# Setup's last stretch of an attention kernel rewritten: key sums with memberships as weights, feature sums on TensorE

## The chip, the cores and the metric

The kernel is one program on one core of a Trainium2 chip. The metric is the device time of that core in microseconds (us). TensorE is called PE, VectorE DVE, ScalarE ACT, GpSimd POOL in the profile; SP issues the transfers. The program is written with explicit semaphores: an engine runs its own instructions in program order, and `wait_ge` holds it until another engine has counted a semaphore up.

## What is computed

A cross-attention block without softmax, then a self-attention block with one; the change is in what the first of them needs once for all rows. Cut to that (H = 8 heads of D = 128, DIM = 256, 32 batches, 256 query rows and 77 context rows in each):

```python
def proj(t):                                   # LayerNorm, then w_in, split in heads
    return heads(layer_norm(t, ln_g, ln_b) @ w_in.T)
f_q, f_k, f_v = proj(q), proj(k), proj(v)      # q: the rows of x, normalized; k = v: the context
k_ratio = 2.0 * jnp.minimum(k_var, 1.0) / (k_var + 1.0)   # k_var: variance over D of a row of f_k
q_flat = (f_q - f_q.mean(-1, keepdims=True)).reshape(H, -1, D)
feat_corr = jnp.einsum('hnd,hne->hde', q_flat, q_flat) / q_flat.shape[1]
decorr_scale = jnp.exp(-5.0 * norm(offdiagonal(feat_corr)) / (D * D))
feats = jnp.concatenate([f_q.mean(axis=(1, 2)), f_k.mean(axis=(1, 2))], axis=-1)
h1 = jnp.maximum(layer_norm(feats @ wp_w1.T + wp_b1, wp_ln_g, wp_ln_b), 0.0)
weights = jax.nn.softmax(h1 @ wp_w2.T + wp_b2, axis=-1)     # three mixing weights for a head
mixed = cw * cosine_sim + vw * cosine_sim * decorr_scale + ww * q_ratio * k_ratio
x = x + jnp.tanh(g_xattn[0]) * (mixed @ f_v @ w_out.T + b_out)
```

## The kernel before

The program has a setup phase and a main phase, two blocks one after the other; the main phase is the same before and after. Setup reads all of x and of the context once, in NG = 4 steps. In a step PE turns the normalized context rows (tile cz, in 5 tiles of 128 rows, CG = 5), ScalarE and VectorE make their fp16 halves (cTh, cTl), PE projects them (`products`: three fp16 matmuls for one fp32 one, high times high, high times low, low times high), VectorE takes the statistics of each head (fst) and from them the ratio that goes into kst; then PE adds 16 tiles of normalized x rows to the gram matrix (gram_ps, with a column of ones that gives the sums of x).

The last stretch of the setup follows those four steps. On each engine it is one list in program order. Its parts:

- wmean and wcT: w_in with the mean of each head's 128 columns taken off (VectorE, L444 to L446).
- krm (L462): for each context row its ratio, spread over the 8 batches of a step and zero where the row isn't of that batch; member is that 0 or 1. 64 columns for a tile of 128 rows (8 batches by 8 heads).
- zs, sums, spread (L476 to L483): the column sums of x and of the context; spread puts them on all 128 columns as weights, so that PE's product with the identity gives them on every partition (L749).
- gram (L487 to L502): the gram matrix with ln_g and ln_b worked in, its lower block ("lower") turned by PE (L753).
- wof: product of two later weights (PE L742, VectorE L505).
- fe, the feature sums (L511 to L515): a multiply of w_in with the spread sums and a reduction, for x and for the context.
- hm = gram x wcT (PE L763), and from it the correlations of four heads each (PE L782, VectorE L532 to L535).
- h1, h1T, logits, dgw, mix: the small network on fe, and its softmax.
- key sums (PE L815, L818): for each batch and head the sum of normalized context rows times ratio. kz is this with ln_g and ln_b, kzTh and kzTl its fp16 halves; "key values" (L861 to L863 on wT and kzT) and the out products (on ku and woutT) follow, and kr goes to HBM as its two halves krh and krl.
- `split_rest(n)`: the low fp16 half of wN, wq, wk, wv and woutT on VectorE (L471), after ScalarE's high half (L642).

PE counts `pe_step` up at each turn, and the other engines wait for its values. The key sums of before take the data as weights:

```python
nc.tensor.matmul(gram_ps[0][:, k * NB * H + i * SB * H:k * NB * H + (i + 1) * SB * H],
                 cz[:, i * CG + t, k * P:(k + 1) * P], weights[t], start=(t == 0), stop=(t == CG - 1))
```

The second argument is the operand that is loaded (128 x 128 here), the third the one that streams (64 columns here), and fp32 matmuls run as two passes, which the profile counts as two instructions.

Of the kernel before, what the change touches and what calls it, by code (L numbers as in the profile page):

```python
# [48 lines left out]
def bc(ap, shape):  # L49
    return ap.to_broadcast(shape)  # L50
# [37 lines left out]
def setup_phase(nc, ctx, w, a):  # L88
# [22 lines left out]
    cz = sb("s_cz", [P, NG * CG, DIM])  # L111
# [20 lines left out]
    spread = sb("s_spread", [P, 2, KT, P])  # L132
# [23 lines left out]
    with ExitStack() as summed:  # L156
        wsum = summed.enter_context(nc.sbuf_tensor("s_wsum", [P, H, DIM], F32))
# [18 lines left out]
    wT_half, wT_split, w_half, w_gated, wof_half = sem("s_wTh"), sem("s_wTs"), sem("s_wh"), sem("s_wg"), sem("s_wofh")  # L176
# [10 lines left out]
    with nc.Block() as block:  # L187
        @block.sync
        def _(sp):
# [25 lines left out]
            with nc.allow_non_contiguous_dma(reason="columns of a few values"):  # L215
# [39 lines left out]
                sp.wait_ge(kr_act, 4)  # L255
# [8 lines left out]
        def _(pool):  # L264
# [14 lines left out]
            nc.gpsimd.memset(fixed[:, 1, 1, :], 0.0).then_inc(consts, 1)  # L279
            nc.gpsimd.memset(member[:], 1.0).then_inc(member_ready, 1)  # L280
            pool.wait_ge(member_ready, 1)
            full_rows, last_rows = member[:, 0:CG - 1, :], member[:, CG - 1, :]
            for n, (rows, pattern, base, sign) in enumerate((
# [5 lines left out]
                pool.wait_ge(member_ready, n + 2)  # L289
# [41 lines left out]
        def _(dve):  # L331
# [94 lines left out]

            dve.wait_ge(wT_half, 1)
# [3 lines left out]
            with dve.Fori(0, NG - 1) as i:  # L431
                count = [0]

                def in_loop(_, ins):
# [9 lines left out]
            link(nc.vector.tensor_reduce(wmean[:], full["wT"][:].rearrange("p k (h d) -> p (k h) d", d=DH), AX.X, ALU.add))  # L444
            link(nc.vector.tensor_scalar(wmean[:], wmean[:], -1.0 / DH, None, ALU.mult))
            link(nc.vector.tensor_tensor(wcT[:].rearrange("p k (h d) -> p (k h) d", d=DH),  # L446
                                         full["wT"][:].rearrange("p k (h d) -> p (k h) d", d=DH),
                                         bc(wmean[:].unsqueeze(2), [P, KT * H, DH]), ALU.add))
            assert done[0] == DVE_LOOPS
            dve.wait_ge(ct_full, NG * CG + START)  # L450
            nc.vector.tensor_reduce(sums[:, :, 1], csums[:].rearrange("p n k -> p k n"), AX.X, ALU.add)
# [3 lines left out]
            link(nc.vector.tensor_scalar(tb[:], tb[:], w["tg"][0:1, 0:1], FV, ALU.mult, ALU.mult))  # L455
            link(nc.vector.tensor_copy(fixed[:, 0, 0, :], tb[:]))
            nc.vector.tensor_tensor(fixed[:, 0, 1, :], tb[:], fixed[:, 0, 0, :], ALU.subtract).then_inc(fixed_ready, 1)
            dve.wait_ge(member_ready, 6)
            dve.wait_ge(rk_ready, 2 * NG + START)
# [5 lines left out]
            last.then_inc(kr_dve, 1)  # L465

            def split_rest(n):
# [7 lines left out]
            dve.wait_ge(pe_step, 1)  # L475
# [4 lines left out]

            for j in range(2):
                for k in range(KT):
                    last = nc.vector.tensor_scalar(spread[:, j, k, :], ones[:], sums[:, k, j:j + 1], None, ALU.mult)  # L483
# [4 lines left out]
            link(last)  # L488
# [4 lines left out]
            dve.wait_ge(pe_step, 3)  # L493
# [7 lines left out]
            dve.wait_ge(pe_step, 4)  # L501
# [8 lines left out]
            for j in range(2):  # L510
                link(nc.vector.tensor_tensor(wsum[:], full["wN"][:], bc(t_ps[0][:, j * DIM:(j + 1) * DIM].unsqueeze(1),  # L511
                                                                        [P, H, DIM]), ALU.mult))
                link(nc.vector.tensor_reduce(fe[:, j, :], wsum[:], AX.X, ALU.add))
            nc.vector.tensor_scalar(fe[:, 0, :], fe[:, 0, :], 1.0 / ROWS, None, ALU.mult)
            tail_link("fe", nc.vector.tensor_scalar(fe[:, 1, :], fe[:, 1, :], 1.0 / CROWS, None, ALU.mult))  # L515
            split_rest(0)

            dve.wait_ge(pe_step, 8)
            link(nc.vector.tensor_tensor(h1[:], t_ps[1][0:H, 0:DH], rows8[:, 0, :], ALU.add))
            link(nc.vector.bn_stats(h1s[:], h1[:]))  # L520
            link(nc.vector.bn_aggr(h1v[:, 0:2], h1s[:]))
            tail_link("h1var", nc.vector.tensor_scalar(h1v[:, 1:2], h1v[:, 1:2], EPS, None, ALU.add))
            dve.wait_ge(pool_step, 3)
# [3 lines left out]
            tail_link("h1", nc.vector.tensor_scalar(h1[:], h1[:], 0.0, None, ALU.max))  # L527

# [57 lines left out]
        def _(act):  # L586
# [1107 lines left out]
```

## Time and profile before

| | us |
|---|---|
| median of 3 runs | 1452.59 (1451.85 to 1452.68) |
| the profiled execution | 1452.54 |
| its span, first to last instruction | 1450.8 |
| PE busy | 1305.6 (90%) |
| VectorE busy | 1138.5 (78%) |
| ScalarE busy | 1023.9 (71%) |
| GpSimd busy | 199.1 (14%) |

Busy shares are those of the whole span. The setup is its first seventh, so the time of the change is to be read from that stretch alone: which engine the others wait for there, and when.

### The profile page before, as it was taken

How to read it: one execution, taken by the hardware profiler on the slowest of the kernel's cores; microseconds unless marked ns; L12 is line 12 of the kernel's file. 1: busy time of each engine (PE TensorE's matmuls, PEld its weight loads, DVE VectorE, ACT ScalarE, POOL GpSimd, SP SyncE). 2: the span in 40 equal slices, each digit the busy share in tenths (PEclk: the TensorE clock that was granted, in tenths of full speed). 3: DMA queues.
4: the chain of work that ended last, by engine and by line, in shares of the span. 5: the costliest groups of instructions: out<-in, count | busy, mean ns of one | idle time of the engine just before them, and what ended most of it. 6: DMA issues, size and time to landing. Idle time of an engine off the chain costs nothing.

```text
span 1450.8 us, 35577 instructions
## 1 busy us (share of the span) xinstructions
PE 1305.6 (90%) x10818; PEld 878.3 (61%) x10818; DVE 1138.5 (78%) x3171; ACT 1023.9 (71%) x3381; POOL 199.1 (14%) x128
## 2 busy tenths in 40 slices
PE   4998838799999999999999999999999999999955
PEld 2565636566666666666666666666666666666621
DVE  5777545578888889888879787979787979797854
ACT  5565113368787878787878787878787878786866
POOL 2343041010202020202020202020202020202000
PEclk9999969899999999999999999999999999999987
DMA  8430001050606060605050505151515141514130
GB/s 265 140 109 18 1 13 46 26 160 5 170 11 166 15 164 16 162 19 160 21 156 25 156 25 147 33 151 30 147 34 142 38 140 41 136 44 130 39 117 15
DMA packets 151433, 124.52 MB, mean 86 GB/s; under 512 B 14462, under 2 KB 139039, under 8 KB 151392
## 3 DMA queue, kind: packets, MB, share of 16 engines
q1 hardware_dynamic: 151392, 124.00, 30.8%
q8 instruction: 22, 0.36, 0.1%
q14 instruction: 19, 0.16, 0.0%
HBM read 87.00 MB, written 25.77 MB: 78 GB/s over the span
## 4 chain that ended last, share of the span: by engine, by line
PE 38%; DVE 18%; issue 14%; ACT 6%; DMA 5%; SPq 3%; DVEq 1%; POOL 1%; ACTq 0%; POOLq 0%
PE work L861 10%; PE work L863 10%; PE work L862 10%; DVE nm L1627 5%; DMA sqE<-sq_rows 4%; PE attended L1347 4%; ACT prob L1437 3%; DVE mTl L1537 3%; PE score L1335 2%; SPq L1180 2%; DVE md L1582 2%; PE work L1242 1%; DVE l2s L1597 1%; DVE norm L1607 1%; DVE norm L1518 1%
## 5 line engine op out<-in xcount | busy, mean ns | idle before, releaser
L1437 ACT ACTIVATE prob<-score,nm 128x256 f32<-128x256 f32 x1024 | 473.2, 480 | 44.6 <-DVE nm L1627 40.4
L1627 DVE TENSOR_REDUCE nm<-score 128x2 f32<-128x512 f32 x512 | 340.2, 683 | 22.2 <-PE score L1335 20.0
L1437 ACT ACTIVATION_READ_ACCUMULATOR prob<-score,nm 128x1 f32 x1024 | 216.7, 212 | 0.0
L1335 PE MATMUL score<-qstack,kstack 128*128 128x256 f16 x1024 | 186.0, 277 | 28.4 <-ACT prob L1437 19.2
L1550 DVE BATCH_NORM_STATS2 qst<-work 128x6 f32<-128x128 f32 x512 | 112.6, 285 | 77.0 <-PE work L863 77.0
L1347 PE MATMUL attended<-prob,vsp 128*32 128x256 f32 x2048 | 139.4, 390 | 4.0 <-DVE vsp L1641 3.2
L1335 PEld LDWEIGHTS score<-qstack,kstack 128*128 128x128 f16 x1024 | 86.6, 98 | 87.7 <-ACT prob L1437 55.5
L861 PE MATMUL work<-woutTh,fvph 128*128 128x256 f16 x384 | 105.0, 273 | 13.7 <-DVE Vpl L1525 12.7
L1482 POOL TENSOR_TENSOR rq<-qft,mhalf 128x32 f32<-128x32 f32 x16 | 86.8, 5428 | 197.0 <-DVEq L1557 197.0
L1422 ACT ACTIVATE v<-work 128x512 f32<-128x512 f32 x32 | 19.1, 597 | 130.4 <-PE work L863 130.4
L862 PE MATMUL work<-woutTl,fvph 128*128 128x256 f16 x384 | 104.7, 273 | 0.0
L863 PE MATMUL work<-woutTh,fvpl 128*128 128x256 f16 x384 | 104.7, 273 | 0.0
L1486 POOL TENSOR_TENSOR l2r<-l2v,mhalf 128x4 f32<-128x4 f32 x16 | 16.1, 1008 | 608.6 <-DVE l2v L1600 608.6
L861 PE MATMUL work<-wTh,xTh 128*128 128x512 f16 x256 | 97.0, 379 | 2.8 <-DVE ql L1537 1.4
L863 PE MATMUL work<-wTh,xTl 128*128 128x512 f16 x256 | 97.0, 379 | 0.0
L862 PE MATMUL work<-wTl,xTh 128*128 128x512 f16 x256 | 97.0, 379 | 0.0
L861 PE MATMUL work<-xTh,Gh 128*128 128x256 f16 (+1 forms) x320 | 88.9, 278 | 6.2 <-DVE md L1582 5.8
L862 PE MATMUL work<-xTl,Gh 128*128 128x256 f16 (+1 forms) x320 | 88.5, 277 | 0.0
L863 PE MATMUL work<-xTh,Gl 128*128 128x256 f16 (+1 forms) x320 | 88.4, 276 | 0.0
L1347 PEld LDWEIGHTS attended<-prob,vsp 128*32 128x32 f32 x2048 | 53.9, 110 | 56.9 <-DVE vsp L1641 17.4
L861 PE MATMUL work<-Vph,mTh 128*128 128x256 f16 (+1 forms) x320 | 87.5, 273 | 0.1
L863 PE MATMUL work<-Vph,mTl 128*128 128x256 f16 (+1 forms) x320 | 87.1, 272 | 0.0
(324 smaller groups left out, 3398.4 us busy)
## 6 DMA issues: line engine op xcount, KB each, us to landing
kstack<-parts SPq DMA_DIRECT2D x256, 64.0 KB, 2.9
qstack<-parts SPq DMA_DIRECT2D x256, 64.0 KB, 2.9
sqE<-sq_rows SPq DMA_DIRECT2D x64, 154.0 KB
s_xin<-in_x SPq DMA_DIRECT2D x8, 1024.0 KB, 6.0
xin<-in_x SPq DMA_DIRECT2D x16, 512.0 KB, 6.7
x2S<-in_x SPq DMA_DIRECT2D x16, 512.0 KB, 7.7
x<-x2S SPq DMA_DIRECT2D x16, 512.0 KB, 3.4
out<-zb SPq DMA_DIRECT2D x16, 512.0 KB, 3.4
```

The lines of the kernel that those rows point to most:

```text
L861: nc.tensor.matmul(out, a["h"][at], b["h"][bt], start=first, stop=False)
L862: nc.tensor.matmul(out, a["h"][at], b["l"][bt], start=False, stop=False)
L863: return nc.tensor.matmul(out, a["l"][at], b["h"][bt], start=False, stop=last)
L1180: sp.dma_start(sqE[lo:hi, t, :], sq_rows[h, :].partition_broadcast(hi - lo)).then_inc(sq_in, 16)
L1335: last = nc.tensor.matmul(sc[n % SC][:, jj * NQ:(jj + 1) * NQ], kstack[:, e, j, b2 * NQ + k * P:b2 * NQ + (k + 1) * P], qstack[:, j, b2 * ...
L1347: last = nc.tensor.matmul(pvb[t][32 * j:32 * j + 32, 0:NQ], vsp[:, e, k, j, :], prob[:, n % PG, k, j, :], start=(e == 0 and k == 0), stop= ...
L1437: nc.scalar.activation(prob[:, g % PG, k, u % 4, :], sc[n % SC][:, jj * NQ:(jj + 1) * NQ], ACT.Exp, bias=nm[:, u:u + 1], accum_out=sums[:, ...
L1482: nc.gpsimd.tensor_tensor(rq[:], qft[:, 0, :, :], w["mhalf"][:].rearrange("p (t h) -> p t h", h=H), ALU.pow).then_inc(rq_ready, 1)
L1537: ins = nc.vector.scalar_tensor_tensor(dst, src, scale, emptied(e, "h")[0], ALU.mult, ALU.subtract)
L1550: last = nc.vector.bn_stats(qst[:, t, 4 * half + h, :], bank(e)[:, h * DH:(h + 1) * DH])
L1582: drain(nc.vector.tensor_tensor(md[0:r, c % 2, 0:n * 2 * P].rearrange("p (t n) -> p t n", n=2 * P), bank(e)[0:r, 0:n * 2 * P].rearrange("p ...
L1627: nc.vector.tensor_reduce(nm[:, 2 * n:2 * n + 2], sc[n % SC][:, :].rearrange("p (u q) -> p u q", q=NQ), AX.X, ALU.max, negate=True).then_i ...
```

## The change

- The key sums exchange their operands: krm (64 columns) is loaded, and cz streams with 256 columns and a 257th of ones, which gives the sum of the ratios that the products with `ones` gave. The result has batches and heads on the partitions, so the gains come in as a row (g_bc, b_bc) on VectorE, and four transposes (kzT) follow. The sums come in two parts: one before hm in the first gram bank, one behind hm in the second.
- The feature sums are PE matmuls: w_in loaded, the two columns of sums streamed. VectorE only scales them. Spread keeps its half for x.
- The gate tanh(g) goes into the scale of woutT's two halves (tgw), and VectorE's multiply of woutT goes.
- wmean and wcT are made ahead of the four steps, before wTl.
- The order in the last stretch is new on all engines; krm no longer waits for the norms that GpSimd makes.

```diff
@@ VectorE, ahead of the four steps @@
+            dve.wait_ge(early, 16 * N_EARLY)
+            link(nc.vector.tensor_reduce(wmean[:], full["wT"][:].rearrange("p k (h d) -> p (k h) d", d=DH), AX.X, ALU.add))
+            link(nc.vector.tensor_scalar(wmean[:], wmean[:], -1.0 / DH, None, ALU.mult))
+            link(nc.vector.tensor_tensor(wcT[:].rearrange("p k (h d) -> p (k h) d", d=DH),
+                                         full["wT"][:].rearrange("p k (h d) -> p (k h) d", d=DH),
+                                         bc(wmean[:].unsqueeze(2), [P, KT * H, DH]), ALU.add))
             dve.wait_ge(wT_half, 1)
...
@@ VectorE, last stretch @@
-            dve.wait_ge(act_step, 1)
-            nc.vector.tensor_scalar(full["woutT"][:], full["woutT"][:], w["tg"][:, 0:1], None, ALU.mult).then_inc(w_gated, 1)
...
-            dve.wait_ge(rk_ready, 2 * NG + START)
...
-                nc.vector.scalar_tensor_tensor(w[name]["l"][:], full[name][:], WS, w[name]["h"][:], ALU.mult, ALU.subtract)
+                nc.vector.scalar_tensor_tensor(w[name]["l"][:], full[name][:], tgw[:, 0:1] if name == "woutT" else WS,
+                                               w[name]["h"][:], ALU.mult, ALU.subtract)
...
+            dve.wait_ge(pe_step, PE_TAIL["fe"])
+            means = t_ps[1][:, DIM:DIM + 2 * H].rearrange("p (h j) -> p j h", j=2)
+            nc.vector.tensor_scalar(fe[:, 0, :], means[:, 0], 1.0 / ROWS, None, ALU.mult)
+            tail_link("fe", nc.vector.tensor_scalar(fe[:, 1, :], means[:, 1], 1.0 / CROWS, None, ALU.mult))
+            dve.wait_ge(pe_step, PE_TAIL["lower"])
             tail_link("lower", nc.vector.tensor_copy(gram[:, 1, 0:P], t_ps[1][:, 0:P]))
...
-                link(nc.vector.tensor_reduce(fe[:, j, :], wsum[:], AX.X, ALU.add))
...
+            dve.wait_ge(kr_act, 2)
+            link(nc.vector.tensor_tensor(kz[:], krs[:, :, 0:DIM], bc(g_bc[:].unsqueeze(1), [P, 2, DIM]), ALU.mult))
+            for n in range(2):
+                last = nc.vector.scalar_tensor_tensor(kz[:, n, :], b_bc[:], krs[:, n, DIM:DIM + 1], kz[:, n, :],
                                                       ALU.mult, ALU.add)
             last.then_inc(kr_dve, 1)
...
@@ ScalarE @@
+            def keep_keys(n):
+                act.wait_ge(pe_step, PE_TAIL[f"keys{n}"])
+                nc.scalar.activation(krs[:, n, :], gram_ps[n][:, 0:DIM + 1], ACT.Copy).then_inc(kr_act, 1)
...
@@ PE @@
+            for h in range(H):
                 for k in range(KT):
+                    last = nc.tensor.matmul(t_ps[1][:, DIM + 2 * h:DIM + 2 * h + 2], full["wT"][:, k, h * DH:(h + 1) * DH],
+                                            sums[:, k, :], start=(k == 0), stop=(k == KT - 1))
+            reached("fe", last)
+
+            def key_sums(n):
+
+                for half in range(2):
+                    i = 2 * n + half
+                    for t in range(CG):
+                        last = nc.tensor.matmul(gram_ps[n][half * SB * H:(half + 1) * SB * H, 0:DIM + 1],
+                                                krm[:, i * CG + t, :, :].rearrange("p b h -> p (b h)"),
+                                                cz[:, i * CG + t, :], start=(t == 0), stop=(t == CG - 1))
+                reached(f"keys{n}", last)
+
+            pe.wait_ge(kr_dve, 1)
+            pe.wait_ge(step, DVE_TAIL["gramg"])
+            key_sums(0)
+            pe.wait_ge(step, DVE_TAIL["fe"])
+            reached("lower", nc.tensor.transpose(t_ps[1][:, 0:P], gram[:, 0, P:DIM], w["ident"][:]))
...
+            key_sums(1)
```

Where the instructions stand shows in the order of each engine (out<-in, shape of the result, xcount of matmuls, not passes). PE before, from the last gram matmul to the start of the second part of the key sums:

```order
L742 MATMUL s_fps<-s_wff,s_woT 128x256 x4
L749 MATMUL s_tps<-ident,s_spread 128x128 x4
L753 MATMUL s_tps<-ident,s_gram 128x128
L763 MATMUL s_fps<-s_wcT,s_gram 128x512 x8
L768 MATMUL s_fps<-ident,s_kst 16x128 x8
L793 MATMUL s_tps<-s_w1T,s_fe 8x128 x2
L782 MATMUL s_gram<-s_hm,s_wcT 128x128 x8
L798 MATMUL s_tps<-ident,s_h 128x8
L782 MATMUL s_gram<-s_hm,s_wcT 128x128 x8
L802 MATMUL s_tps<-s_w2T,s_h1T 8x3
L768 MATMUL s_fps<-ident,s_kst 16x128 x8
L815 MATMUL s_gram<-s_krm,s_cz 128x64 x10
```

PE after, the same place:

```order
L746 MATMUL s_fps<-s_wff,s_woT 128x256 x4
L752 MATMUL s_tps<-ident,s_spread 128x128 x2
L756 MATMUL s_tps<-s_sums,s_wT 128x2 x16
L765 MATMUL s_gram<-s_cz,s_krm 64x257 x10
L774 MATMUL s_tps<-ident,s_gram 128x128
L776 MATMUL s_tps<-s_w1T,s_fe 8x128 x2
L787 MATMUL s_fps<-s_wcT,s_gram 128x512 x8
L765 MATMUL s_gram<-s_cz,s_krm 64x257 x10
L793 MATMUL s_fps<-ident,s_kst 16x128 x8
L816 MATMUL s_tps<-ident,s_h 128x8
L807 MATMUL s_gram<-s_hm,s_wcT 128x128 x8
L821 MATMUL s_tps<-s_w2T,s_h1T 8x3
```

The feature sums (s_sums, s_wT) and the first key sums (s_cz, s_krm) now stand ahead of the hm matmuls (s_wcT, s_gram), the second ones behind them, and h1's matmul ahead of hm.

VectorE before, at the end of the four steps, from wmean to the gram's first operation:

```order
L444 TENSOR_REDUCE s_wmean<-s_wT 128x16
L445 TENSOR_SCALAR s_wmean<-s_wmean 128x16
L446 TENSOR_TENSOR s_wcT<-s_wT,s_wmean 128x2048
L451 TENSOR_REDUCE s_sums<-s_csums 128x2
L454 TENSOR_SCALAR s_woutT<-s_woutT,tg 128x2048
L455 TENSOR_SCALAR s_tb<-s_tb,tg 1x256
L456 CAST s_fixed<-s_tb 1x256
L457 TENSOR_TENSOR s_fixed<-s_tb,s_fixed 1x256
L462 TENSOR_TENSOR s_krm<-s_kst,s_member 128x320 x4
L476 COPY s_zs<-s_gram 128x1
```

VectorE after, at the start of the setup, from the first shift to the first x statistics:

```order
L356 SCALAR_TENSOR_TENSOR s_cnm<-s_cmv,s_crs 128x5
L428 TENSOR_REDUCE s_wmean<-s_wT 128x16
L429 TENSOR_SCALAR s_wmean<-s_wmean 128x16
L430 TENSOR_TENSOR s_wcT<-s_wT,s_wmean 128x2048
L434 SCALAR_TENSOR_TENSOR wTl<-s_wT,wTh 128x2048
L361 BN_STATS s_xst<-s_xin 128x6 x8
```

The wmean and wcT operations went from the first place to the second, ahead of wTl.

VectorE before, from the second correlation to the out products:

```order
L546 TENSOR_REDUCE s_lg<-s_lg 8x1
L548 COPY s_dec<-s_tps 128x8
L471 SCALAR_TENSOR_TENSOR wkl<-s_wk,wkh 128x512
L553 SCALAR_TENSOR_TENSOR s_kz<-s_fps,bcol,s_kz 128x256 x2
L557 RECIPROCAL s_lg<-s_lg 8x1
L558 TENSOR_SCALAR s_lg<-s_lg 8x3
L560 TENSOR_SCALAR s_dgw<-ident,s_lg 8x8 x3
L471 SCALAR_TENSOR_TENSOR wvl<-s_wv,wvh 128x512
L471 SCALAR_TENSOR_TENSOR woutTl<-s_woutT,woutTh 128x2048
L566 TENSOR_TENSOR s_kzTl<-s_kz,s_kzTh 128x512
L568 SCALAR_TENSOR_TENSOR wofl<-s_wo,wofh 128x2x256
```

VectorE after, from the second correlation to the out products:

```order
L523 TENSOR_TENSOR s_fc<-s_gram,s_off 128x512
L525 TENSOR_TENSOR s_fc<-s_fc 128x512
L526 TENSOR_REDUCE s_fcs<-s_fc 128x4
L545 SCALAR_TENSOR_TENSOR s_kzTl<-s_fps,s_kzTh 128x512
L548 RECIPROCAL s_lg<-s_lg 8x1
L549 TENSOR_SCALAR s_lg<-s_lg 8x3
L551 TENSOR_SCALAR s_dgw<-ident,s_lg 8x8 x3
L554 COPY s_dec<-s_tps 128x8
L466 SCALAR_TENSOR_TENSOR wvl<-s_wv,wvh 128x512
L466 SCALAR_TENSOR_TENSOR woutTl<-s_woutT,s_tgw,woutTh 128x2048
L558 SCALAR_TENSOR_TENSOR s_kul<-s_fps,s_kuh 128x256
```

The split of wk and the kz operation are gone from here (they stand ahead of the correlations now), kzTl stands ahead of the softmax tail and of the splits, and kul right behind woutTl.

## Rows read from the trace of the kernel before

**Rows 1.** Timeline of GpSimd at the change of phase: start, us, engine, line, operation
```profile
203.50 2.93 POOL L1469 MEMSET fvph<- 128x3391 f16 x1 [19.71 <-POOLq L187]
```

**Rows 2.** Windows: us; busy us and count of PE, PEld, DVE, ACT, POOL; clock; DMA
```profile
160.00:180.00 20.00, 17.43 (x142) 16.84 (x142) 7.20 (x19) 1.01 (x1) 0.54 (x1) 0.91 0.01 1
```

**Rows 3.** Timeline of ScalarE (ACT), start of the setup
```profile
12.18 1.91 ACT L589 ACTIVATE wTh<-s_wT 128x2048 f16<-128x2048 f32 x1 [10.09 <-DMA s_bbc<-in_ln_b]
```

**Rows 4.** Timeline of VectorE (DVE), start of the setup
```profile
14.13 2.29 DVE L428 SCALAR_TENSOR_TENSOR wTl<-s_wT,wTh 128x2048 f16<-128x2048 f32 x1 [4.52 <-ACT wTh L589]
16.34 2.70 DVE L361 BATCH_NORM_STATS2 s_xst<-s_xin 128x6 f32<-128x256 f32 x8
```

**Rows 5.** Timeline of PE in the setup; a bracket is idle time and releaser
```profile
33.20 0.38 PE L861 MATMUL s_fps<-wTh,s_cTh 128*128 128x512 f16 x1 [1.11 <-DVE s_fst L379]
...
139.23 0.92 PE L735 MATMUL s_gram<-s_zeros 1*128 1x257 f32 x4
140.08 1.99 PE L742 MATMUL s_fps<-s_wff,s_woT 128*128 128x256 f32 x8
...
163.05 3.60 PE L782 MATMUL s_gram<-s_hm,s_wcT 128*128 128x128 f32 x16
...
167.59 2.34 PE L815 MATMUL s_gram<-s_krm,s_cz 128*128 128x64 f32 x20
169.77 1.28 PE L818 MATMUL s_fps<-s_krm,s_ones 128*128 128x64 f32 x10
...
187.49 0.22 PE L861 MATMUL s_fps<-s_kzTh,wTh 128*128 128x32 f16 x1 [2.92 <-DVE s_kzTl L566]
...
191.53 0.40 PE L861 MATMUL s_fps<-woutTh,s_kuh 128*32 128x256 f16 x1 [1.00 <-DVE s_kul L579]
```

**Rows 6.** Timeline of VectorE, last stretch of the setup
```profile
133.18 2.28 DVE L444 TENSOR_REDUCE s_wmean<-s_wT 128x16 f32<-128x2048 f32 x1
...
135.71 2.29 DVE L446 TENSOR_TENSOR s_wcT<-s_wT,s_wmean 128x2048 f32<-128x2048 f32 x1
...
140.36 1.68 DVE L462 TENSOR_TENSOR s_krm<-s_kst,s_member 128x320 f32<-128x320 f32 x4
141.97 0.14 DVE L476 COPY s_zs<-s_gram 128x1 f32<-128x1 f32 x1
...
148.16 2.29 DVE L511 TENSOR_TENSOR s_wsum<-s_wN,s_tps 128x2048 f32<-128x2048 f32 x1
...
162.88 0.69 DVE L532 TENSOR_TENSOR s_fc<-s_gram,s_off 128x512 f32<-128x512 f32 x1
...
182.98 0.14 DVE L557 RECIPROCAL s_lg<-s_lg 8x1 f32<-8x1 f32 x1
...
184.54 2.29 DVE L471 SCALAR_TENSOR_TENSOR woutTl<-s_woutT,woutTh 128x2048 f16<-128x2048 f32 x1
186.74 0.69 DVE L566 TENSOR_TENSOR s_kzTl<-s_kz,s_kzTh 128x512 f16<-128x512 f32 x1
...
191.05 0.42 DVE L579 SCALAR_TENSOR_TENSOR s_kul<-s_fps,s_kuh 128x256 f16<-128x256 f32 x1 [2.44 <-ACT s_kuh L677]
198.76 2.28 DVE L582 SCALAR_TENSOR_TENSOR s_krl<-s_fps,s_krh 32x2048 f16<-32x2048 f32 x1 [7.29 <-ACT s_krh L680]
```

**Rows 7.** Windows of the last stretch; the third number from the end is the clock
```profile
142.00:146.20 4.20, 1.23 (x9) 0.97 (x8) 3.96 (x17) 0.60 (x1) 0.00 (x0) 1.00 0.00 0
149.93:154.65 4.72, 4.72 (x13) 2.09 (x12) 4.65 (x3) 1.02 (x1) 0.00 (x0) 1.00 0.00 0
163.30:166.70 3.40, 3.40 (x18) 3.16 (x17) 2.51 (x6) 0.00 (x0) 0.00 (x0) 0.50 0.01 2
167.50:180.90 13.40, 13.40 (x123) 13.40 (x121) 1.59 (x4) 1.01 (x1) 0.00 (x0) 1.00 0.01 1
187.50:190.50 3.00, 3.00 (x48) 2.85 (x48) 1.04 (x5) 0.00 (x0) 0.00 (x0) 0.50 0.00 0
191.50:196.70 5.20, 5.17 (x24) 3.45 (x24) 0.00 (x0) 0.00 (x0) 0.00 (x0) 0.50 0.00 0
```

More of the change, by code:

```diff
@@ L775, in turn_keys @@
                         last = turn_stats(f_ps[0:2 * H, i, t * P:(t + 1) * P], i, t)
-                last.then_inc(pe_step, 1)
+                reached(f"turned{n}", last)
             def correlate(a):
@@ L840, in _ @@
             for i in range(NG):
                 last = turn_stats(gram_ps[1][0:2 * H, i * P:(i + 1) * P], i, CG - 1)
-            last.then_inc(pe_step, 1)
-            pe.wait_ge(step, DVE_TAIL["dgw"])
-            nc.tensor.matmul(t_ps[0][:, 0:3 * H], ones[0:H, :], dgw[:].rearrange("p a h -> p (a h)"),
-                             start=True, stop=True).then_inc(pe_step, 1)
-            key_values()
+            reached("last", last)
+            pe.wait_ge(kr_dve, 3)
+            for h in range(H):
+                for k in range(KT):
+                    rows = {half: kzT[half][:, k, :].rearrange("p (b h) -> p b h", h=H) for half in "hl"}
+                    last = products(nc, f_ps[:, 1, h * NB:(h + 1) * NB], w["wT"], (ALL, k, slice(h * DH, (h + 1) * DH)),
+                                    rows, (ALL, ALL, h), k == 0, k == KT - 1)
@@ new lines, in _ @@
+            last.then_inc(kr_pe, 1)
+            pe.wait_ge(step, DVE_TAIL["dgw"])
+            pe.wait_ge(step, DVE_TAIL["dec"])
+            reached("mix", nc.tensor.matmul(t_ps[0][:, 0:3 * H], ones[0:H, :], dgw[:].rearrange("p a h -> p (a h)"),
+                                            start=True, stop=True))
+            pe.wait_ge(kr_dve, 4)
+            pe.wait_ge(kT_ready, 2)
+            for h in range(H):
+                last = products(nc, f_ps[0:NB, h // 2, h % 2 * DIM:(h % 2 + 1) * DIM], ku, (ALL, h), w["woutT"], (ALL, h))
@@ L850 @@
+            last.then_inc(kr_pe, 1)
 STEP_LINKS = 4 + 8 + 7
 DVE_LOOPS = 4 + 3 + NG * STEP_LINKS - 4
-_TAIL = ["bias", "biash", "zs", "zg", "sums", "spread", "gramg", "gramb", "bu", "gram", "lower", "wof", "wx", "xmean", "wc", "cmean", "fe",
-         "h1add", "h1bn", "h1aggr", "h1var", "h1norm", "h1g", "h1b", "h1", "fcmask0", "fcsq0", "fcsum0", "h1T",
-         "fcmask1", "fcsq1", "fcsum1", "ladd", "lmax", "dec", "lrec", "lscale", "dgw"]
+_TAIL = ["zs", "zg", "sums", "spread", "gramg", "gramb", "bu", "gram", "fe", "lower", "wof",
+         "h1add", "h1bn", "h1aggr", "h1var", "h1norm", "h1g", "h1b", "h1", "h1T", "kzg", "fcmask0", "fcsq0", "fcsum0",
+         "ladd", "lmax", "fcmask1", "fcsq1", "fcsum1", "lrec", "lscale", "dgw", "dec"]
@@ L855 @@
 DVE_TAIL = {name: DVE_LOOPS + 1 + n for n, name in enumerate(_TAIL)}
+_TURNS = ["gram", "wof", "spread", "fe", "keys0", "lower", "h1", "hm0", "hm1", "keys1", "turned0", "h1T", "corr0", "logits",
+          "corr1", "turned1", "kzT", "norms", "last", "mix"]
+PE_TAIL = {name: 1 + n for n, name in enumerate(_TURNS)}
 def products(nc, out, a, at, b, bt, first=True, last=True):
```

222 lines of the change are left out of this document (95 added, 127 removed).

## The prediction

> **What bounds the kernel now.** The change lies wholly in the setup, the first 203.5 of 1450.8 us; the main phase after it begins only when setup's last store has landed (GpSimd's first memset of it, 203.50 [rows 1]), so what setup gains or loses moves the rest as a block. I then read the busy time by stretch: between 160 and 180 us PE is busy 17.43 of 20 us and VectorE 7.20 [rows 2], so PE is the bound there. The timelines then give the order. The tail begins where PE ends the gram matrix (L735) at about 140.08 [rows 5]; VectorE is late for it and touches it at 141.97, behind krm [rows 6]. Then VectorE is the bound for the feature sums (four operations of 2.29 us from 148.16) and PE for the key sums from 167.59 to 180.9, and the reader is to see that VectorE then still has two splits to do (182.98 to 186.74) before kzTl, which releases the first key-values matmul at 187.49. The out products start at 191.53 behind kul. Everything behind that point (24 products, krh, krl, the store) stays as it is, so I build the new start of the out products and compare it with 191.53.
>
> **The front, which gets longer.** The wcT block (L444 to L446: 2.28, about 0.2 and 2.29 us, 4.8 in all [rows 6]) goes ahead of wTl. The weights are there at 12.18, when ScalarE starts wTh [rows 3]; VectorE idles until 14.13 and then makes wTl [rows 4]. Now it works from 12.18 to 17.0 and wTl starts at 17.0: 2.9 us late. Is that absorbed? Behind wTl on VectorE stand the row statistics of the first x block (16.34), on which the normalization, the lowers and so PE wait; PE itself waits for VectorE at 33.20 [rows 5]. I see no wait on a transfer between, so I take all 2.9; the bounds are 0 (all absorbed) and 4.8 (nothing of the block hidden). The loops and the gram's end come 2.9 later, at 142.98.
>
> **The hand-over to the tail.** On VectorE the block (4.8), the gate of woutT and the fixed rows (all of them between 133.18 and krm's start at 140.36) go from in front of krm; krm itself is 1.68 [rows 6] and needs no reciprocal norms from GpSimd any more. It is done by about 138, so VectorE now waits for the gram: it starts at 143.1 and not at 141.97, 1.1 us later than before. ScalarE's woutTh now starts 10 us earlier; nothing waits for it, since its split is the last, so that is worth nothing here.
>
> **PE's queue in the tail.** A full 128-column fp32 weight load with few moving columns costs one pass 0.11 us (167.59 to 169.77 is 20 passes, twice 0.11 for each fp32 matmul [rows 5]). A pass of 512 columns costs 0.43 us at full clock (11 starts in 4.72 us [rows 7]), and one of 256 at most 0.25 (8 in 1.99 [rows 5]); for the new passes of 257 columns I take 0.22, between half of 0.43 and 0.25.
> Removed: 120 passes, 13.4 us, of the old key sums [rows 5, 7], and of the spread half its passes. Added: the feature sums, 16 matmuls = 32 passes of 2 columns, 3.5 us; the key sums in two parts of 20 passes, 4.4 us each; four transposes. The 2-column pass is not in the trace: the nearest from below is 0.06 us (the fp16 key-values products, 48 from 187.49 in 3.0 us [rows 5, 7]), which gives 1.9 us; from above the slow-clock pass of L782, 16 in 3.60 or 0.225 [rows 5], which gives 7.2. It loads the same fp32 weights as L815, so 0.11.
> PE then runs without a wait that I can find: wof 1.9, feature sums 3.5, first key sums 4.4, the hm matmuls 16 x 0.43 = 6.9, second key sums 4.4, first correlation 16 x 0.11 = 1.8, and 18 small passes (spread, lower, h1, the turned keys, h1T) 2.0. The sum is 24.9, with 0.3 for hand-overs 25.2: 168.2. VectorE's gram work, 4.5 us, hides under PE's feature sums and first key sums; wNl (2.3 us) and two small splits hide under hm. If PE's stretch were shorter than about 14 us, those would show.
>
> **Then VectorE again.** Two correlations of three 0.69 us operations [rows 6], the logits between (0.3) and kzTl 0.7 make 5.2: 173.4, with hand-overs 173.9. kz (about 1.6: three operations of the 0.69 us kind and shorter) fits before the first correlation, since the second key sums end at about 165.4. Key-values products start at 174.0 and not at 187.49. Behind kzTl stand the softmax tail and one split (182.98 to 184.54, 1.6), the copy of dec 0.2 and woutTl 2.2 (184.54 to 186.74) [rows 6]: 177.9. PE needs 3.0 us for the products and ScalarE 0.4 for kuh, 177.5, so kul waits for woutTl by 0.4. With kul's 0.42 the out products start at 178.5. Against 191.53 that is **13.0 us** of gain at full clock, the front's 2.9 us already taken off.
> The DMA of the reciprocal norms now goes out some 3 us earlier and the fixed rows with it, both long before krh; they cost nothing.
>
> **The clock.** PE's granted clock is 0.50 in 3.40 us from 163.30, 1.00 from 167.50 to 180.90, and 0.50 again in both last product stretches [rows 7]. It fell after stretches such as 142.0 to 146.2, where PE was busy 1.23 of 4.20 us. Of the stretch from 187.5 to 190.5 PE counts 3.00 busy, with 32-column matmuls, and stays at 0.50. The new feature sums are 3.5 us of passes with 2 columns, less array work than any of these. I hold it likelier than not that the clock falls once by them, and that 3.4 us of work then run at 1.2 GHz: half of 3.4, 1.7 us, is lost. Gain 13.0 - 1.7 = 11.3. The last products are taken at 0.50 as before.
> The Trainium skill, page TensorE: Matmul & The Clock Gate, section What's actually happening, says that the gate is set by how busy PE has been, and that activity releases it. Taken by PE's busy time the feature sums would count as work and the clock would stay up: the sum would be 13.0 and not 11.3. The trace's 187.5 stretch, busy and yet at 0.50, does not bear that reading out, but no row shows a fall under it.
>
> **Rivals.**
> (A) The clock holds through the feature sums: 1452.6 - 13.0 = **1439.6**. For it: it holds over 13.4 us of 64-column key sums. 30%.
> (B) The front's 2.9 us are absorbed in the loops: 1452.6 - 15.9 = 1436.7, or 1438.4 with one fall. Against it: PE waits for VectorE in each block. 7%.
> (C) The last products run at full clock, because PE's wait before the key-values products (2.92 us for kzTl [rows 5]) becomes shorter: half of 5.2 us comes off, 1438.7 with one fall. Against it: the 32-column products stand before them as they did, and no rise came then. 9%.
> (D) The clock falls twice or more, or the 257-column passes cost as much as two (8.8 us more): 1443 to 1450. 11%.
> (E) Slower: the feature sums put the clock down and the key sums, whose weights fill half of the columns, do not bring it back. From 145.4 to 173 PE has some 25 us of work at full clock; each us of it done at 0.50 costs one more. It decides from 13.0 us of such work on, and with all of it the time is 1452.6 + 12 = 1464.6. For it: 5.2 us at 0.50 from 191.5 with 256 columns. Against it: it rose at 166.7 and held through 64 columns [rows 7]. 3%.
>
> **How the numbers follow.** The profiled run took 1452.54 us, the median of the runs is 1452.59, so differences of the trace hold for the median. The forecast (one fall, 40%) is 1452.6 - 11.3 = 1441.3 us. Range: down to (B) and (C) without their tails, 1437.0, and up into (D), 1446.0. Within 0.2% (2.9 us) is about what a measurement of this kernel can't tell from no change. Faster by more: all cases but (E) and the end of (D), 0.95; the same 0.02; slower 0.03.
>
> **What would show it.** The second VectorE wTl at 17 us; L735 ending near 143; a granted clock of 0.50 for one stretch within 146 to 154; PE without idle from 145 to 170; VectorE idle about 5 us before the gram and again before h1T; the first key-values matmul near 174 (176 with a fall) and the first out product near 178.5 (180). It would be wrong if 257-column passes cost far over 0.22, if VectorE's waits in the reordered tail (it now waits for lower only behind the key sums, with wof, h1 and wNl queued behind) reach PE, or if the loops take up the front's delay.

## The result, and the profile after

The changed kernel took 1435.99 us in the median of 4 runs (1433.1 to 1438.16), the kernel before 1452.22 (1448.39 to 1452.68): ratio 0.9893, 95% interval 0.9868 to 0.9917, so 12.1 to 19.2 us faster. Over all later runs too the means are 1452.8 us (43 runs, standard deviation 2.4) and 1437.4 us (13 runs, 2.7): 15.4 us, with a standard error of 0.8. The forecast was 1441.3, between 1437.0 and 1446.0. The direction and the mechanism in the setup were right; the time came out 1.0 us below the range.

The profiled execution took 1433.1 us, its span is 1431.4. GpSimd's timeline of it shows the end of the setup, where before it was at 203.50 [rows 1]:

```profile
188.03 2.93 POOL L1479 MEMSET fvph<- 128x3391 f16 x1 [13.17 <-POOLq L186]
```

So 15.5 us of the 19.4 by which the two spans differ come from the setup, and 3.9 from the main phase, whose program is the same.

VectorE's timeline of the front, for [rows 4]:

```profile
12.29 2.29 DVE L428 TENSOR_REDUCE s_wmean<-s_wT 128x16 f32<-128x2048 f32 x1 [2.41 <-DMA s_bbc<-in_ln_b]
...
17.15 2.29 DVE L434 SCALAR_TENSOR_TENSOR wTl<-s_wT,wTh 128x2048 f16<-128x2048 f32 x1
19.36 2.70 DVE L361 BATCH_NORM_STATS2 s_xst<-s_xin 128x6 f32<-128x256 f32 x8
```

The block runs from 12.29, and wTl starts 3.0 us later than before, as forecast (2.9).

VectorE's timeline of the last stretch, for [rows 6]:

```profile
133.43 1.70 DVE L455 TENSOR_TENSOR s_krm<-s_kst,s_member 128x320 f32<-128x320 f32 x4
135.04 0.19 DVE L460 TENSOR_REDUCE s_sums<-s_csums 128x2 f32<-128x40 f32 x1
140.25 0.16 DVE L470 COPY s_zs<-s_gram 128x1 f32<-128x1 f32 x1 [5.02 <-PE s_gram L739]
...
146.24 0.15 DVE L496 TENSOR_SCALAR s_fe<-s_tps 128x8 f32<-128x8 f32 x1
151.74 0.29 DVE L498 COPY s_gram<-s_tps 128x128 f32<-128x128 f32 x1 [5.35 <-PE s_tps L774]
...
170.91 0.69 DVE L545 SCALAR_TENSOR_TENSOR s_kzTl<-s_fps,s_kzTh 128x512 f16<-128x512 f32 x1 [0.19 <-ACT s_kzTh L665]
...
173.28 2.34 DVE L466 SCALAR_TENSOR_TENSOR woutTl<-s_woutT,s_tgw,woutTh 128x2048 f16<-128x2048 f32 x1
175.54 0.41 DVE L558 SCALAR_TENSOR_TENSOR s_kul<-s_fps,s_kuh 128x256 f16<-128x256 f32 x1
```

krm is done at 135, then VectorE waits 5.0 us for the gram, and 5.4 us for lower behind the feature sums. kul follows woutTl without a gap.

PE's timeline of the last stretch, for [rows 5]:

```profile
139.29 0.92 PE L739 MATMUL s_gram<-s_zeros 1*128 1x257 f32 x4
...
142.41 3.63 PE L756 MATMUL s_tps<-s_sums,s_wT 128*128 128x2 f32 x32
145.97 5.40 PE L765 MATMUL s_gram<-s_cz,s_krm 128*64 128x257 f32 x20
...
152.10 7.13 PE L787 MATMUL s_fps<-s_wcT,s_gram 128*128 128x512 f32 x16
159.16 3.74 PE L765 MATMUL s_gram<-s_cz,s_krm 128*64 128x257 f32 x20
...
171.66 0.22 PE L871 MATMUL s_fps<-s_kzTh,wTh 128*128 128x32 f16 x1
...
176.01 0.40 PE L871 MATMUL s_fps<-woutTh,s_kuh 128*32 128x256 f16 x1 [0.76 <-DVE s_kul L558]
```

PE runs without a gap from the gram to the second correlation. The first key sums take 5.4 us and the second 3.7, with the same 20 passes. The last gram matmul starts at 139.29, and not 2.9 us behind the 139.23 of before. From there to the first out product are 36.7 us, where [rows 5] give 52.3.

Windows of the changed kernel; the clock is the third number from the end, for [rows 7]:

```profile
142.50:145.90 3.40, 3.40 (x33) 3.40 (x31) 1.81 (x6) 0.27 (x1) 0.00 (x0) 1.00 0.02 5
147.40:150.70 3.30, 3.30 (x13) 1.96 (x12) 0.00 (x0) 0.00 (x0) 0.00 (x0) 0.50 0.00 0
159.30:162.80 3.50, 3.50 (x20) 2.12 (x19) 0.00 (x0) 0.99 (x1) 0.00 (x0) 1.00 0.00 0
176.00:181.00 5.00, 4.99 (x24) 3.43 (x24) 2.01 (x8) 0.00 (x0) 0.00 (x0) 0.50 0.12 16
```

The 32 two-column passes run at full clock; 1.3 us behind them the clock falls to 0.50 for 3.4 us, within the first key sums. The second key sums run at 1.00, and the out products at 0.50 as before.

### The profile page after: what moved, and what is told of

Same layout as the page of the kernel before. It is cut to its first block, busy times and chain, and to the rows that moved or that the text cites. A ratio compares the mean times of both kernels' runs of the same rounds, so it can differ in the third digit from the quotient of the medians.

```text
span 1431.4 us, 35480 instructions
## 1 busy us (share of the span) xinstructions
PE 1296.1 (91%) x10770; PEld 870.6 (61%) x10770; DVE 1127.5 (79%) x3165; ACT 1022.2 (71%) x3382; POOL 200.7 (14%) x129
## 4 chain that ended last, share of the span: by engine, by line
PE 39%; DVE 18%; issue 14%; ACT 6%; DMA 5%; SPq 2%; DVEq 1%; POOL 1%; ACTq 0%; POOLq 0%
PE work L871 11%; PE work L873 11%; PE work L872 11%; DVE nm L1637 6%; DMA sqE<-sq_rows 4%; PE attended L1357 4%; ACT prob L1447 3%; DVE mTl L1547 2%; PE score L1345 2%; SPq L1190 2%; DVE md L1592 2%; PE work L1252 1%; DVE l2s L1607 1%; DVE norm L1617 1%; DVE norm L1528 1%
## 5 line engine op out<-in xcount | busy, mean ns | idle before, releaser
L1447 ACT ACTIVATION_READ_ACCUMULATOR prob<-score,nm 128x1 f32 x1024 | 220.6, 215 | 0.0
```

What stands on the lines that cost most here:

```text
L1447: nc.scalar.activation(prob[:, g % PG, k, u % 4, :], sc[n % SC][:, jj * NQ:(jj + 1) * NQ], ACT.Exp, bias=nm[:, u:u + 1], accum_out=sums[:, ...
```

## The experiments

**Where the front's delay went.** The gram's last matmul came at the same time in both first profiles, though everything in front of it began 2.9 us late. Four runs ask why: both kernels again, the block put back in the changed kernel, and the block alone moved in the kernel before.

The block (wmean and the operations after it to wcT) put back (wc_back), its first two operations shown:

```diff
-            dve.wait_ge(early, 16 * N_EARLY)
-            link(nc.vector.tensor_reduce(wmean[:], full["wT"][:].rearrange("p k (h d) -> p (k h) d", d=DH), AX.X, ALU.add))
-            link(nc.vector.tensor_scalar(wmean[:], wmean[:], -1.0 / DH, None, ALU.mult))
...
             dve.wait_ge(wT_half, 1)
...
             tiles(NG - 1, straight, False)
+            link(nc.vector.tensor_reduce(wmean[:], full["wT"][:].rearrange("p k (h d) -> p (k h) d", d=DH), AX.X, ALU.add))
+            link(nc.vector.tensor_scalar(wmean[:], wmean[:], -1.0 / DH, None, ALU.mult))
...
             assert done[0] == DVE_LOOPS
```

The block alone moved (front_only) is the same edit the other way round, in the kernel before.

> The kernel before, unchanged, for a second profile. Theory 1 (the granted clock's slow stretches in the four steps fall where they fall by chance in each execution, and that hid the front's 2.9 us): the steps' total time at clock 0.50 differs from the first profile's 17 us, and the end of the gram (L735) moves with it, by up to 3 us to either side of 139.2. Theory 2 (the delay of the front itself moves the steps to where the clock falls less): the total is 17 us again and L735 starts within 0.5 us of 139.2.

> The changed kernel, unchanged, for a second profile and a time. Theory 1: L739 starts somewhere from 139 to 143.5, in step with the time at clock 0.50 in the four steps (6.9 us in the first profile). Theory 2: 139.3 again. Either way VectorE is idle behind krm until the gram, and the first out product comes 36 to 38 us behind L739's start (36.7 in the first profile). Time 13 to 17 us below the kernel before.

> The changed kernel with the three wmean/wcT operations put back behind the four steps, where VectorE was idle for 5.0 us: they take 4.8 there. Theory 1 (the front costs its 2.9 us, hidden in the first profile by chance): 2.9 us faster than after_again in the median of the rounds, wTl starts at about 14.1. Theory 2 (the front costs nothing or the later start even helps): the same time as after_again or up to 3 us slower.

> The kernel before with only the three wmean/wcT operations moved ahead of wTl. VectorE then reaches the gram about 2 us sooner than PE ends it, so PE's end binds. By theory 1: steps 2.9 us later, VectorE's lateness at the gram (1.8 us) gone: 1.1 us slower than the kernel before. By theory 2: 1.8 us faster, or more. VectorE idle for about 3 us in front of the gram only if it is freed of the block.

Windows of the four steps, first of the kernel before in its first profile, then of before_again, then of front_only:

```profile
16.00:136.00 120.00, 107.07 (x517) 66.91 (x518) 91.58 (x415) 75.20 (x206) 41.80 (x19) 0.93 0.41 129
```

```profile
16.00:136.00 120.00, 105.08 (x534) 68.06 (x535) 94.01 (x417) 75.00 (x205) 44.65 (x19) 0.97 0.41 128
```

```profile
16.00:136.00 120.00, 102.28 (x517) 65.37 (x518) 93.97 (x418) 76.69 (x207) 41.70 (x19) 0.97 0.41 129
```

PE's timeline at the last gram matmul of before_again and of front_only:

```profile
136.38 0.92 PE L735 MATMUL s_gram<-s_zeros 1*128 1x257 f32 x4
```

```profile
139.29 0.92 PE L736 MATMUL s_gram<-s_zeros 1*128 1x257 f32 x4
```

With the clock at a mean of 0.97 in both, the block in front costs 139.29 - 136.38 = 2.9 us. The first profile of the kernel before had 0.93 there: 17.1 us at 0.50, by windows of 1 us added up, against 6.8 in before_again. It is the odd one in where the gram ends: six profiles of the kernel before have the last gram matmul at 139.23, 136.38, 136.81, 136.60, 136.66 and 136.80, five of the changed kernel at 139.29, 138.65, 138.64, 139.49 and 138.81. The means are 137.1 and 139.0; without the odd one the front costs 2.3 us. It is not absorbed in the steps, or by 0.6 us at most. Theory 1 stands in its main point, that the first profile of before hid the delay by chance. But the end of the gram does not simply move with the time at 0.50: with the same code in the steps it came at 136.28 both in wc_back (3.4 us at 0.50) and in filled_turns (10.3 us), at 136.66 in before_p5 (10.3 us). It was late only in the first profile of before (17.1 us, 139.23) and in mixed (13.6 us, 138.25), and these two alone of the nine profiles with that code have 6.8 us at 0.50 in one piece, at 57 to 64 us. That this piece is the cause is not shown.

wc_back has the block where VectorE was idle, as its VectorE timeline shows (block, then the gram's first operation):

```profile
130.22 2.28 DVE L444 TENSOR_REDUCE s_wmean<-s_wT 128x16 f32<-128x2048 f32 x1
...
137.23 0.16 DVE L469 COPY s_zs<-s_gram 128x1 f32<-128x1 f32 x1 [0.37 <-PE s_gram L738]
```

Its last gram matmul starts at 136.28, but the feature and key sums then met 6.8 us at 0.50, where the first profile of the changed kernel had 3.4. Its time was 1441.11 us in the median, 0.9909 of before (0.9886 to 0.9933), against 1437.87 and 0.9902 (0.9879 to 0.9925) for after_again. Theory 1 asked for 2.9 us less and the median is 3.2 us more, so by its time this expectation failed; the two intervals overlap almost wholly, and the run can't tell 2.9 us either way. front_only took 1454.97, 1.0014 of before (0.9994 to 1.0034); theory 1 asked for 1.1 us more, which lies inside (so does no change at all), and theory 2's 1.8 us less lies outside. In its profile setup ends at 200.95, where the kernel before, without its odd profile, has 199.9 in the mean, which agrees with theory 1. VectorE is less late there, and not in time: krm still waits 3.65 us for GpSimd's norms, and the hm matmuls start 6.3 us behind the last gram matmul's start, where before had 7.6.

**What the feature sums cost, and what drops the clock.** One kernel (fe_wide, the diff) streams 64 columns where 2 were streamed; the other (fe_one) has the same edit with `range(1)` for `range(H)`, so only the first head's four passes are left:

```diff
             for h in range(H):
                 for k in range(KT):
-                    last = nc.tensor.matmul(t_ps[1][:, DIM + 2 * h:DIM + 2 * h + 2], full["wT"][:, k, h * DH:(h + 1) * DH],
-                                            sums[:, k, :], start=(k == 0), stop=(k == KT - 1))
+                    last = nc.tensor.matmul(t_ps[1][:, DIM:DIM + 64], full["wT"][:, k, h * DH:(h + 1) * DH],
+                                            spread[:, k, 0:64], start=(k == 0), stop=(k == KT - 1))
```

> The changed kernel, with the feature sums' 16 matmuls streaming 64 columns (of the spread sums of x) where 2 were streamed; the sums of single heads and of the context are left out, so its output is not the reference's. Its weight loads stay, so a pass stays at 0.11 us and the 32 take 3.6. If the 2-column passes are what drops the clock (it fell 1.3 us behind their end in the first profile, 3 us behind their start in the second), there is no stretch at 0.50 between 142 and 152, and the first key sums take 3.7 us like the second. If it is something else (the gap ahead, chance), the stretch stays and the first key sums take 5 us or more.

> The changed kernel with one head's feature sum in place of eight: 14 of the 16 matmuls are left out, so its output is not the reference's. If PE's queue binds from the gram to the second key sums, as the prediction's sum has it, the way from the last gram matmul's start to the first out product is shorter by 28 passes x 0.11 = 3.1 us, and by 1.7 more if the clock then holds: 36.7 becomes 33.6 or 31.9. If VectorE's gram work or its splits bound it instead, less than 1.5 us comes off.

PE's timeline and windows of fe_wide:

```profile
142.26 3.68 PE L756 MATMUL s_tps<-s_spread,s_wT 128*128 128x64 f32 x32
145.87 3.75 PE L765 MATMUL s_gram<-s_cz,s_krm 128*64 128x257 f32 x20
```

```profile
142.30:145.80 3.50, 3.50 (x34) 3.50 (x32) 1.85 (x6) 0.31 (x1) 0.00 (x0) 1.00 0.02 5
145.90:149.50 3.60, 3.60 (x21) 2.24 (x20) 0.24 (x2) 0.00 (x0) 0.00 (x0) 1.00 0.00 0
```

The same 32 passes take the same 3.6 us (PEld, the weight load, is busy in all of the 3.50 us with 64 columns as in all of the 3.40 with 2, so it sets the pace, 0.11 a pass), the clock stays at 1.00, and the first key sums take 3.7 us. From the last gram matmul to the first out product are 35.1 us. In all eight profiles in which the 2-column passes stand in one run (five of the changed kernel, one each of wc_back, keys_turns and filled_turns) the clock fell within or just behind them: for 3.4 us in four of them, for 6.8 in the other four. fe_wide is one profile; in fe_one, and in mixed below, no such run of passes is left, and the clock did not fall there either. In fe_one the way from the last gram matmul to the first out product is 32.0 us:

```profile
142.10 0.56 PE L756 MATMUL s_tps<-s_spread,s_wT 128*128 128x64 f32 x4
142.59 3.75 PE L765 MATMUL s_gram<-s_cz,s_krm 128*64 128x257 f32 x20
```

That is 3.1 us shorter than in fe_wide for 28 passes less: PE's queue bounds this stretch, as the sum had it.

**The key sums' passes.** 257 columns were taken at 0.22 us a pass; 20 take 3.7 us, 0.185. They are ten passes on output partitions 0 to 63 and then ten on 64 to 127. An order in which the halves take turns tests that:

```diff
-                for half in range(2):
-                    i = 2 * n + half
-                    for t in range(CG):
+                for t in range(CG):
+                    for half in range(2):
+                        i = 2 * n + half
```

> The changed kernel with the two halves of each key sum taking turns (tile by tile) where they came one after the other. In the profiles 20 passes took 3.7 us at full clock, with starts 0.2 us apart at both ends and 0.07 where the second half (output partitions 64 to 127) follows the first (0 to 63). If passes on different column halves run side by side, and only those of one half wait for each other, each key sum takes about 20 x 0.11 = 2.2 us: 1.5 us less for each, 3 us for both, with PE bound there. If the order doesn't matter, 3.7 us again and no change.

PE's timeline of keys_turns:

```profile
146.87 4.01 PE L765 MATMUL s_gram<-s_cz,s_krm 128*64 128x257 f32 x20
...
158.68 2.40 PE L765 MATMUL s_gram<-s_cz,s_krm 128*64 128x257 f32 x20
```

The second key sums, at full clock, take 2.4 us instead of 3.7, 0.12 a pass: passes on different halves of the output partitions overlap more than those on one half. In both orders a single pass is recorded with 0.38 us. (The Trainium skill, page TensorEngine Tiling (Array Packing), section Key Properties, says that different tiles can execute weight loads and matmuls in parallel; the 0.12 us a pass agrees.) The first take 4.0 in spite of a slow stretch of 3.4 us (5.4 in the changed kernel). The way is 34.0 us. The time, 1436.65 us or 0.9887 (0.987 to 0.9903), is that of the changed kernel within its interval.

**All of it together.** filled_turns has the turns, the block back behind the steps, and the splits of wv and woutT in front of the wait for lower:

```diff
+            split_rest(3)
+            split_rest(4)
             dve.wait_ge(pe_step, PE_TAIL["lower"])
...
-            split_rest(3)
-            split_rest(4)
             dve.wait_ge(kr_act, 4)
```

> The changed kernel with the halves in turns, the wmean/wcT operations back behind the four steps (VectorE idle 5.0 us there) and the splits of wv and woutT moved from behind the softmax tail to where VectorE waits for lower (5.4 us idle). By the sum: 2.9 (front) + up to 3.0 (key sums) + 0.4 (kul no longer waits for woutTl) = 6 us faster than the changed kernel. Two things can eat it: the splits (2.8 us) may reach past lower once the first key sums are 1.5 us shorter, and the clock's slow stretches, worth about 1.7 us each, fall by chance.

Its VectorE timeline: the block, the gram's first operation, woutTl and kul:

```profile
130.23 2.28 DVE L444 TENSOR_REDUCE s_wmean<-s_wT 128x16 f32<-128x2048 f32 x1
...
137.24 0.16 DVE L469 COPY s_zs<-s_gram 128x1 f32<-128x1 f32 x1 [0.35 <-PE s_gram L738]
...
144.03 2.35 DVE L465 SCALAR_TENSOR_TENSOR woutTl<-s_woutT,s_tgw,woutTh 128x2048 f16<-128x2048 f32 x1
...
169.66 0.42 DVE L557 SCALAR_TENSOR_TENSOR s_kul<-s_fps,s_kuh 128x256 f16<-128x256 f32 x1 [2.59 <-ACT s_kuh L666]
```

The idle 5.0 us are used up but for 0.35, and kul waits for kuh alone. The first out product is at 170.1 and setup ends at 181.5 (186.7 to 189.9 in five profiles of the changed kernel). The time is 1432.07 us, 0.9861 of before (0.9843 to 0.988): the lowest median of all, 4.6 us below keys_turns and 3.9 below the changed kernel's 1435.99. Against the changed kernel's mean over all 13 runs, 1437.4, its mean of 4 is 5.3 us lower with a standard error of 1.3, near the expected 6. The intervals of the two ratios overlap (0.9868 to 0.988), so that it beats the changed kernel is likely, not certain.

**A miss.** mixed deals the feature sums' passes out between the key tiles, so that no run of narrow passes is left (its `key_tile(0, h)` is one key matmul, halves in turns, and `key_sums(0, H)` makes the rest); the two waits of the key sums move ahead of the feature sums with it, and otherwise it is filled_turns:

```diff
+            for h in range(H):
+                key_tile(0, h)
                 for k in range(KT):
...
             reached("fe", last)
...
-            key_sums(0)
+            key_sums(0, H)
```

> filled_turns with the feature sums' matmuls dealt out between the tiles of the first key sums: four 2-column passes, then a key tile of two 257-column passes, and so on, the last two tiles behind them. The passes are the same ones. If the run of 2-column passes is what drops the clock, it now stays at 1.00 from the gram to the second key sums and the way from the last gram matmul's start to the first out product is 1.7 us shorter than in filled_turns (33.9): 32.2. If the key tiles no longer overlap one another between the narrow passes, up to 1.4 us of that is lost again: 33.6. By time: 1 to 2 us below filled_turns (0.986 of before), which the rounds may not tell.

The moved waits cost little: PE starts 3.21 us behind the last gram matmul's start, against 3.13 in filled_turns.

Its PE timeline, first four groups, and its windows:

```profile
141.46 0.65 PE L756 MATMUL s_gram<-s_cz,s_krm 128*64 128x257 f32 x2
142.04 0.61 PE L770 MATMUL s_tps<-s_sums,s_wT 128*128 128x2 f32 x4
142.58 0.65 PE L756 MATMUL s_gram<-s_cz,s_krm 128*64 128x257 f32 x2
143.16 0.61 PE L770 MATMUL s_tps<-s_sums,s_wT 128*128 128x2 f32 x4
```

```profile
142.30:145.80 3.50, 3.50 (x22) 2.29 (x21) 1.00 (x3) 0.00 (x0) 0.00 (x0) 1.00 0.00 0
145.90:149.50 3.60, 3.60 (x20) 2.33 (x21) 0.00 (x0) 0.00 (x0) 0.00 (x0) 1.00 0.02 5
```

The clock stays at 1.00, as expected. But a key tile of two passes and four narrow passes now take 1.12 us together (142.58 - 141.46), where four weight-bound passes and two in turns would take 4 x 0.11 + 2 x 0.12 = 0.68. The way is 36.4 us against 33.9 in filled_turns, and the upper expectation of 33.6 was too low as well. Of the 0.44 us more in each group 0.13 is the lost overlap of the halves (a key tile's two passes are one matmul on one half; by the times of the two orders that is 2 x 0.185 = 0.37 and not 0.24); 0.31 is left. A further 0.30 us, once, is PE's wait for lower in the hm matmuls. (The Trainium skill, page TensorEngine Tiling (Array Packing), section Key Properties, says that a change of tiling mode drains TensorE; each group here has two such changes, and the 0.31 us that are left would fit that. No run isolates both; in fe_one the four passes and the change to 64-column weights take 0.49 us, only 0.05 more than 4 x 0.11.) It took 1434.75 us, 0.9864 (0.9846 to 0.9881).

**The main phase.** Its share of the gain was open, so more profiles of the two kernels were taken, with no edit.

> The kernel before, a third profile. In the first two the last gram matmul starts at 139.23 (17 us at clock 0.50 in the four steps) and 136.38 (6.8 us). If the first was the odd one, and 136.4 is where the kernel usually is, this one gives 136.3 to 137.0 and a first out product at 188.6 to 189.3; if both are common, either. The main phase behind setup took 1247.3 and 1249.6 us and should lie between 1243 and 1253.

> The kernel before, a fourth profile, with the same expectation as the third: last gram matmul at 136.3 to 137.0 if the first profile was the odd one.

> The changed kernel, a third profile. Last gram matmul at 138.7 to 139.3 (2.4 to 2.9 us behind the usual one of before), first out product 36.7 us later with one slow stretch in the first key sums. Main phase: 1243.4 us and 1248.2 in the first two; if the first was chance, about 1249.

> The kernel before, a fifth profile. Main phase (from GpSimd's first memset of it to the end) 1250 us if the new setup shortens it, 1248 to 1249 as the common mean if it is scatter; single profiles scatter by 2.5 us, so only the means over all of them count. Setup ends at 199.4 to 199.7 in three of four.

> The kernel before, a sixth profile, expectation as for the fifth.

> The changed kernel, a fourth profile. Main phase 1246 if it is shorter behind the new setup, 1248 to 1249 if that was scatter. Setup ends at 186.7 to 188.9.

> The changed kernel, a fifth profile, expectation as for the fourth.

From each profile: the start of GpSimd's first memset of the main phase, and the span less that.

| profile | setup ends | main phase |
|---|---|---|
| before, 6 profiles | 203.50, 199.41, 199.50, 199.66, 200.98, 200.05 | 1247.3, 1249.6, 1252.5, 1251.4, 1244.5, 1251.6 |
| changed, 5 profiles | 188.03, 186.69, 188.86, 189.86, 188.97 | 1243.4, 1248.2, 1247.2, 1247.1, 1249.6 |

The setup is shorter by 200.5 - 188.5 = 12.0 us in the mean. The main phase means are 1249.5 and 1247.1, 2.4 apart with a standard error of 1.6. The low clock doesn't make this difference: added up over windows of 2 us, the main phase has 56.6 to 73.9 us at 0.50 before, 64.5 in the mean, and 62.4 to 67.3 in the changed kernel, 65.4 in the mean. Behind the other kernels with the new last stretch it took 1252.5 (wc_back), 1250.0 (fe_wide), 1249.5 (fe_one), 1250.3 (keys_turns), 1246.7 (filled_turns) and 1250.0 (mixed), behind front_only 1253.0. All 11 profiles with the new last stretch have 1248.6 in the mean and all 7 with the old one 1250.0, 1.4 apart with a standard error of 1.4. These speak for scatter, but don't settle it.

## Why the prediction was right or wrong

- *The setup is where it happens, PE binds its last stretch, and VectorE's lateness goes.* Right: PE has no gap until the second correlation, and fe_one took off what its missing passes cost.
- *The front is 2.9 us later and is not absorbed.* Right: 2.9 at like clock, 2.3 in the mean of profiles without the odd one. Rival B (absorbed) looked right in the first pair of profiles and was not; the kernel before had been measured there with 17 us of slow clock in its steps. That profile was also the basis of the sum: the forecast put the gram's last matmul at 142.1 (139.23 + 2.9), and it came at 139.0, because before it is usually at 136.7. For the first out product the forecast had 180.2 with one fall, and five profiles gave 175.3 to 177.8; the kernel before has it at 189.1 in the mean of six and not at 191.53. So the absolute times were 2 to 5 us too late, and the difference, before to after, was hardly touched: 12.4 us in these means, against 11.3 forecast.
- *The way from the gram to the out products.* The forecast's 178.5 - 142.1 = 36.4 us at full clock and 38.1 with one fall; measured 35.1 with no fall (fe_wide), 36.7 with one, 38.3 with two. The term that was mis-sized is the 257-column pass: 0.22 taken, 0.185 measured, 1.4 us for 40 of them. The 2-column pass (0.11) and the hm pass (0.43 taken, 7.06 us for 16 or 0.44 measured) were right.
- *The clock falls once by the feature sums.* Right that it falls: it did in all five profiles, and fe_wide, one profile with 64 columns in the same passes, has no fall. It stayed down for 3.4 us in two of the five and for 6.8, the two falls of rival D, in three. Rival A (it holds) did not come up. PE counts 3.40 of 3.40 us busy in the narrow passes, and the clock falls behind them. The Trainium skill (page TensorE: Matmul & The Clock Gate, section What's actually happening) says that "activity releases the throttle"; read by PE's busy time, this trace does not agree.
- *C, D, E.* The out products began at 0.50 in all five, and the clock rose only at their end, if at all (against C): in the changed kernel it was at 1.00 for the first passes of the key-values products, where before it was at 0.50, and fell at the latest 0.4 us behind them. Two falls did come (part of D), at a cost of 1.6 us more (38.3 against 36.7), which is where D's lower end of 1443 lies. E did not happen: the clock was back at 1.00 before the first key sums ended, in all five.
- *The step that failed* is the one in "What bounds the kernel now", that what setup gains moves the rest as a block, together with "differences of the trace hold for the median". The setup gained 12.0 us in the mean of the profiles (standard error 0.8), inside the 11.3 to 13.0 of the sum. The timed gain was 15.4 (standard error 0.8) in the means of all runs, and 16.2 between the two medians of the first. The main phase is no block: its time varies from 1243.4 to 1253.0 us between executions, most of its 16 passes being 72 to 75 us long in no pattern that I could find, and the range had no term for that. Whether the 3.4 us between 12.0 and 15.4 are this scatter, or the main phase is shorter behind the new setup, stays open: the profiles have 2.4 us of it with a standard error of 1.6, which doesn't tell. That the four timed runs fell below the range is in part chance: their median is 1.0 us below its end, single runs scatter by 2.7, and the mean of all 13, 1437.4, lies just inside. The gain of 15.4 against the 11.3 of the forecast is clear of it.

## What to carry to other kernels

A profile is one execution: before a sum is built on its absolute times, look how much of a stretch it spent at the low clock, and compare like with like. Behind a run of matmuls with very few columns, look at the granted clock even where PE counts as busy: here the work behind 32 passes of 2 columns lost it in 8 of 8 profiles, and in the one profile with 64 columns in these passes neither the clock fell nor did they take longer (3.6 us). Matmuls that fill different halves of the output partitions should take turns, and be kept in one run.

## What the runs showed of the hardware

- fp32 passes with 128-column weights and 2 or 64 moving columns take the same 0.11 us, but only the 2-column run was followed by a fall of the clock to 0.50 (8 of 8 profiles with 2 columns, 0 of 1 with 64). A fall cost 1.6 us (35.1, 36.7 and 38.3 us of way with none, 3.4 us and 6.8 us at 0.50).
- The 48 fp16 passes of the key-values products, 32 columns each and begun at 1.00, were followed by a fall too: within them or at most 0.4 us behind them, in all 11 profiles with the new last stretch. What decides there is not tested.
- Matmuls with 64-column weights and 257 moving columns, on the two halves of the output partitions in turn, take 0.12 us a pass (2.4 us for 20); one half after the other the same 20 passes take 3.7 us.
- Alternating 64-column and 128-column weights every few passes cost 0.44 us a group, eight times in mixed, so more in all than the fall that it avoided (1.6 us). 0.13 of it is lost overlap; the rest is not isolated.
- In the four steps (16 to 136 us) the low clock came in stretches of 3.4 or 6.8 us, and by the old last products for longer (183.9 to 197.0 in the first profile). Where they fall differs from execution to execution: in the four steps they took from 3.4 to 17.1 us in profiles of the same code there.
